# Another order of tasks and PSUM banks for a software-pipelined two-layer kernel on one core

## The reference, cut to what matters

```
xn = layernorm(x)
s  = tanh(beta * (spin + global + softmax(spin W_J spin^T) spin)),  spin = xn W_spin + b
g  = silu(sigmoid(xr W_r) * (relu(xk W_k)^2 W_v)),                  xr, xk mix a token with the one before
x  = x + s * g
xn = layernorm(x)
s  = retention over 16 heads (decaying causal scores, row sums of |scores|, rms norm), gated, W_o
g  = silu(soft mixture of 8 experts x 64 slots: logits, two softmaxes, slots, w1, gelu, w2, combine)
x  = x + s * g
```

## Time and profile before

| | us |
|---|---|
| median of 3 runs | 1090.27 (1090.27 to 1090.41) |
| the profiled execution | 1089.83 |
| its span, first to last instruction | 1088.0 |
| TensorE, VectorE, ScalarE, GpSimd busy | 1048.5, 919.0, 806.6, 387.3 |
| mean granted TensorE clock, of 2.4 GHz | 0.995 |

### The profile page before, as it was taken

How to read it: one execution, slowest core, us unless ns; L and a number is a source line. 1 busy time by engine, 2 the same in 40 slices (tenths; PEclk the granted TensorE clock), 3 DMA queues, 4 the chain that set the end, 5 groups by cost and what they waited for, 6 DMA issues and landing times.

```text
span 1088.0 us, 27272 instructions
## 1 busy us (share of the span) xinstructions
PE 1048.5 (96%) x10244; PEld 828.0 (76%) x10244; DVE 919.0 (84%) x1818; ACT 806.6 (74%) x1434; POOL 387.3 (36%) x555
## 2 busy tenths in 40 slices
PE   5799999999999999999999999999999999999997
PEld 3478787787878778787786877778787787877866
DVE  3788888988889888997988889888998888989785
ACT  4487877778777786877778777887777868777775
POOL 2432533334343332433335233343433324333240
PEclk9899999999999999999999999999999999999999
DMA  6000000000000000000000000000000000000000
GB/s 257 11 11 2 11 11 2 21 2 11 11 2 21 2 11 11 3 20 2 21 1 12 11 2 20 2 11 11 2 21 2 15 7 11 12 1 12 2 11 11
DMA packets 18463, 16.85 MB, mean 15 GB/s; under 512 B 800, under 2 KB 17440, under 8 KB 18080
## 3 DMA queue, kind: packets, MB, share of 16 engines
q1 hardware_dynamic: 18336, 15.12, 4.3%
HBM read 10.93 MB, written 4.19 MB: 14 GB/s over the span
## 4 chain that ended last, share of the span: by engine, by line
PE 90%; DVE 5%; issue 4%; POOL 1%; ACT 1%; DVEq 0%; POOLq 0%; ACTq 0%
PE bank L969 11%; PE bank L979 11%; PE bank L1023 10%; PE bank_s L1000 7%; PE bank L989 6%; PE bank L960 5%; PE bank L930 5%; PE bank L952 3%; PE bank L910 3%; PE bank L1038 3%; PE bank L825 3%; PE bank L1030 3%; PE bank L876 3%; PE bank L923 3%; PE bank L856 2%
## 5 line engine op out<-in xcount | busy, mean ns | idle before, releaser
L326 POOL TENSOR_TENSOR ret_abs<-ret_abs 128x512 f32<-128x512 f32 x128 | 168.3, 1315 | 435.9 <-ACT ret_abs L479 435.9
L659 DVE TENSOR_TENSOR ret<-bank_s,k_sb 128x1536 f32<-128x1536 f32 x128 | 224.1, 1751 | 5.0 <-PE bank L1023 2.2
L479 ACT ACTIVATE ret_abs<-ret 128x1536 f32<-128x1536 f32 x128 | 189.1, 1477 | 0.5 <-DVE ret L659 0.5
L474 ACT ACTIVATE hact<-hact 128x512 f32<-128x512 f32 x128 | 80.1, 626 | 86.5 <-DVE hact L728 86.1
L979 PE MATMUL bank<-w_sb,hact 128*128 128x128 f32 x1024 | 132.0, 277 | 0.0
L969 PE MATMUL bank<-slotsT,w_sb 128*128 128x128 f32 x1024 | 130.7, 278 | 0.9 <-ACT slotsT L469 0.9
L979 PEld LDWEIGHTS bank<-w_sb,hact 128*128 128x128 f32 x1024 | 124.1, 192 | 8.9 <-ACT hact L474 4.3
L969 PEld LDWEIGHTS bank<-slotsT,w_sb 128*128 128x128 f32 x1024 | 120.6, 192 | 10.2 <-issue 6.6
L1023 PE MATMUL bank<-ret,vrow 128*32 128x256 f32 (+1 forms) x2048 | 108.3, 329 | 0.0
L728 DVE TENSOR_TENSOR hact<-bank,v_sb 128x512 f32<-128x512 f32 x128 | 87.6, 685 | 11.7 <-PE bank L979 8.2
L333 POOL TENSOR_SCALAR dT<-dT,drec 128x256 f32<-128x256 f32 x128 | 64.5, 517 | 91.7 <-DVE drec L723 91.7
(11 more groups left out here) (143 smaller groups left out, 2307.1 us busy)
## 6 DMA issues: line engine op xcount, KB each, us to landing
x_sb<-x SPq DMA_DIRECT2D x16, 256.0 KB, 2.8
w_sb<-w SPq DMA_DIRECT2D x2, 2048.0 KB, 14.2
out<-attn SPq DMA_DIRECT2D x16, 256.0 KB, 2.3
v_sb<-vectors SPq DMA_DIRECT2D x1, 705.0 KB, 7.5
k_sb<-consts SPq DMA_DIRECT2D x1, 538.0 KB, 6.3
w_sb<-weights SPq DMA_DIRECT2D x1, 512.0 KB, 5.0
w_sb<-weights SPq DMA_DIRECT2D x1, 320.0 KB, 3.3
slot_sb<-slot_rows SPq DMA_DIRECT2D x1, 256.0 KB, 3.5
```

Of the source, the lines that this page charges most:

```text
L326: pool.tensor_tensor(both[:, :, P:SEQ], both[:, :, P:SEQ], both[:, :, SEQ:3 * P], ALU.add)\
L474: act.activation(hact[:, e % 2], hact[:, e % 2], ACT.Gelu).then_inc(ready["hg"].sem, 1)
L479: act.activation(ret_abs[:, q % MR], ret[:, q % MR], ACT.Abs).then_inc(ready["ab"].sem, 1)
L659: dve.tensor_tensor(ret[:, q % MR], bank_s[:, :, 0:3 * P], causal.unsqueeze(1).broadcast_to([P, Q, 3 * P]), ALU.mult)\
```

## The change

Both tables are written anew, and nothing else is touched: no function, no instruction and no transfer. In `ORDER` every engine's list has the same tasks as before in another sequence. Six tasks of TensorE change their age: quad 7, h 4, eo 2, eo 3 and h 5 go from 2 to 1, ms 2 from 1 to 2. On VectorE eoc 0, hb 3, ret 7, hb 4 and eoc 1, on ScalarE dsq 2 and hg 3 go from 2 to 1, and on GpSimd rstd2 from 1 to 0. `BANK` gives most tasks another bank. The new tables were laid out with longer durations for VectorE, ScalarE and GpSimd.

```diff
@@ -51,53 +51,53 @@
 ORDER = {
-    "PE": [("quad", 7, 2), ("h", 4, 2), ("eo", 2, 2), ("eo", 3, 2), ("h", 5, 2), ("h", 6, 2), ("eo", 4, 2),
-           ("h", 7, 2), ("eo", 5, 2), ("xn2T", 0, 1), ("g", 6, 2), ("g", 7, 2), ("qk", 0, 1), ("eo", 6, 2),
-           ("ms", 3, 2), ("eo", 7, 2), ("qk", 1, 1), ("gT", 0, 1), ("vg", 0, 1), ("xn3T", 0, 1), ("out", 0, 2),
-           ("quad", 0, 1), ("out", 1, 2), ("LT", 0, 1), ("LT", 1, 1), ("quad", 1, 1), ("LT", 2, 1), ("xnT", 0, 0),
-           ("LT", 3, 1), ("gT", 1, 1), ("vg", 1, 1), ("s", 0, 0), ("quad", 2, 1), ("g", 0, 1), ("g", 1, 1),
-           ("DT", 0, 1), ("e", 0, 0), ("global", 0, 0), ("r", 0, 0), ("o", 0, 2), ("quad", 3, 1), ("o", 1, 2),
-           ("k", 0, 0), ("ms", 0, 1), ("mxT", 0, 1), ("score", 0, 0), ("DT", 1, 1), ("score", 1, 0),
-           ("quad", 4, 1), ("g", 2, 1), ("g", 3, 1), ("PT", 0, 0), ("rB", 0, 1), ("DT", 2, 1), ("quad", 5, 1),
-           ("DT", 3, 1), ("srow", 0, 0), ("ms", 1, 1), ("PT", 1, 0), ("slots", 0, 1), ("slots", 1, 1),
-           ("v", 0, 0), ("local", 0, 0), ("h", 0, 1), ("quad", 6, 1), ("g", 4, 1), ("g", 5, 1), ("h", 1, 1),
-           ("h", 2, 1), ("h", 3, 1), ("eo", 0, 1), ("eo", 1, 1), ("ms", 2, 1)],
-    "DVE": [("eoc", 0, 2), ("hb", 3, 2), ("rx", 2, 2), ("ret", 7, 2), ("hb", 4, 2), ("eoc", 1, 2), ("hb", 5, 2),
-            ("xn2", 0, 1), ("hb", 6, 2), ("hb", 7, 2), ("stat", 0, 0), ("xn3", 0, 1), ("den", 3, 2), ("ug", 3, 2),
-            ("eoc", 2, 2), ("rx", 3, 2), ("qkc", 0, 1), ("eoc", 3, 2), ("qkc", 1, 1), ("vgc", 0, 1), ("z", 0, 2),
-            ("gated", 0, 2), ("ret", 0, 1), ("z", 1, 2), ("xn", 0, 0), ("LTm", 0, 1), ("gated", 1, 2),
-            ("ret", 1, 1), ("LTm", 1, 1), ("mx", 0, 1), ("LTm", 2, 1), ("vgc", 1, 1), ("mix", 0, 0), ("zg", 0, 2),
-            ("drec", 0, 1), ("mx", 1, 1), ("ret", 2, 1), ("den", 0, 1), ("gbias", 0, 0), ("mx", 2, 1),
-            ("ug", 0, 1), ("drec", 1, 1), ("attn", 0, 2), ("ret", 3, 1), ("attn", 1, 2), ("rx", 0, 1),
-            ("rmax", 0, 1), ("drec", 2, 1), ("LTm", 3, 1), ("sg", 0, 2), ("smax", 0, 0), ("smax", 1, 0),
-            ("drec", 3, 1), ("ret", 4, 1), ("den", 1, 1), ("ug", 1, 1), ("x2", 0, 2), ("cs", 0, 1), ("ka", 0, 0),
-            ("rx", 1, 1), ("cs", 1, 1), ("cs", 2, 1), ("srowc", 0, 0), ("ret", 5, 1), ("srec", 0, 0), ("rv", 0, 0),
-            ("cs", 3, 1), ("field", 0, 0), ("hb", 0, 1), ("rvg", 0, 0), ("prod", 0, 0), ("x1", 0, 0),
-            ("ret", 6, 1), ("hb", 1, 1), ("stat2", 0, 0), ("ug", 2, 1), ("den", 2, 1), ("hb", 2, 1)],
-    "ACT": [("dsq", 2, 2), ("hg", 3, 2), ("hg", 4, 2), ("ab", 7, 2), ("hg", 5, 2), ("ce", 3, 2), ("xn2Tc", 0, 1),
-            ("hg", 6, 2), ("usq", 3, 2), ("dsq", 3, 2), ("hg", 7, 2), ("ln", 0, 2), ("gTb", 0, 1), ("rs", 0, 2),
-            ("xn3Tc", 0, 1), ("LTc", 0, 1), ("zt", 0, 2), ("LTc", 1, 1), ("ab", 0, 1), ("LTc", 2, 1),
-            ("xnTc", 0, 0), ("ab", 1, 1), ("LTc", 3, 1), ("DTe", 0, 1), ("gTb", 1, 1), ("sT", 0, 0), ("DTe", 1, 1),
-            ("usq", 0, 1), ("Dc", 0, 1), ("eTc", 0, 0), ("ab", 2, 1), ("tr", 0, 0), ("dsq", 0, 1), ("DTe", 2, 1),
-            ("kr", 0, 0), ("sgT", 0, 0), ("ab", 3, 1), ("Dc", 1, 1), ("DTe", 3, 1), ("P", 0, 0), ("P", 1, 0),
-            ("usq", 1, 1), ("PTc", 0, 0), ("rBc", 0, 1), ("Dc", 2, 1), ("dsq", 1, 1), ("Dc", 3, 1), ("ab", 4, 1),
-            ("ce", 0, 1), ("slc", 0, 1), ("ce", 1, 1), ("PTc", 1, 0), ("slc", 1, 1), ("tv", 0, 0), ("ab", 5, 1),
-            ("ce", 2, 1), ("sp", 0, 0), ("hg", 0, 1), ("hg", 1, 1), ("usq", 2, 1), ("ab", 6, 1), ("hg", 2, 1)],
-    "POOL": [("add", 6, 2), ("rstd2", 0, 1), ("rnorm", 0, 1), ("add", 7, 2), ("rstd", 0, 0), ("km", 0, 1),
-             ("km", 1, 1), ("km", 2, 1), ("add", 0, 1), ("mixa", 0, 0), ("add", 1, 1), ("dn", 0, 1), ("km", 3, 1),
-             ("dn", 1, 1), ("add", 2, 1), ("km", 4, 1), ("km", 5, 1), ("add", 3, 1), ("dn", 2, 1), ("km", 6, 1),
-             ("km", 7, 1), ("dn", 3, 1), ("add", 4, 1), ("add", 5, 1)],
+    "PE": [("h", 6, 2), ("ms", 2, 2), ("eo", 4, 2), ("h", 7, 2), ("eo", 5, 2), ("xn2T", 0, 1), ("g", 6, 2),
+           ("g", 7, 2), ("xn3T", 0, 1), ("qk", 0, 1), ("qk", 1, 1), ("eo", 6, 2), ("ms", 3, 2), ("eo", 7, 2),
+           ("LT", 0, 1), ("quad", 0, 1), ("out", 0, 2), ("out", 1, 2), ("LT", 1, 1), ("gT", 0, 1), ("xnT", 0, 0),
+           ("vg", 0, 1), ("quad", 1, 1), ("gT", 1, 1), ("LT", 2, 1), ("o", 0, 2), ("vg", 1, 1), ("LT", 3, 1),
+           ("s", 0, 0), ("DT", 0, 1), ("quad", 2, 1), ("g", 0, 1), ("g", 1, 1), ("mxT", 0, 1), ("e", 0, 0),
+           ("k", 0, 0), ("quad", 3, 1), ("DT", 1, 1), ("rB", 0, 1), ("ms", 0, 1), ("DT", 2, 1), ("o", 1, 2),
+           ("score", 0, 0), ("global", 0, 0), ("score", 1, 0), ("quad", 4, 1), ("g", 2, 1), ("g", 3, 1),
+           ("PT", 0, 0), ("r", 0, 0), ("DT", 3, 1), ("quad", 5, 1), ("srow", 0, 0), ("PT", 1, 0), ("v", 0, 0),
+           ("slots", 0, 1), ("slots", 1, 1), ("local", 0, 0), ("ms", 1, 1), ("h", 0, 1), ("h", 1, 1),
+           ("quad", 6, 1), ("g", 4, 1), ("g", 5, 1), ("eo", 0, 1), ("h", 2, 1), ("eo", 1, 1), ("h", 3, 1),
+           ("quad", 7, 1), ("eo", 2, 1), ("h", 4, 1), ("eo", 3, 1), ("h", 5, 1)],
+    "DVE": [("hb", 5, 2), ("xn2", 0, 1), ("rx", 2, 2), ("hb", 6, 2), ("xn3", 0, 1), ("eoc", 2, 2), ("hb", 7, 2),
+            ("stat", 0, 0), ("ug", 3, 2), ("qkc", 0, 1), ("den", 3, 2), ("qkc", 1, 1), ("xn", 0, 0), ("rx", 3, 2),
+            ("eoc", 3, 2), ("ret", 0, 1), ("z", 0, 2), ("gated", 0, 2), ("z", 1, 2), ("LTm", 0, 1), ("LTm", 1, 1),
+            ("mx", 0, 1), ("vgc", 0, 1), ("drec", 0, 1), ("ret", 1, 1), ("gated", 1, 2), ("attn", 0, 2),
+            ("zg", 0, 2), ("vgc", 1, 1), ("LTm", 2, 1), ("mx", 1, 1), ("mix", 0, 0), ("mx", 2, 1), ("drec", 1, 1),
+            ("drec", 2, 1), ("ret", 2, 1), ("rmax", 0, 1), ("den", 0, 1), ("ug", 0, 1), ("ret", 3, 1),
+            ("rx", 0, 1), ("LTm", 3, 1), ("attn", 1, 2), ("sg", 0, 2), ("gbias", 0, 0), ("smax", 0, 0),
+            ("drec", 3, 1), ("smax", 1, 0), ("ka", 0, 0), ("ret", 4, 1), ("ug", 1, 1), ("srec", 0, 0),
+            ("cs", 0, 1), ("cs", 1, 1), ("den", 1, 1), ("srowc", 0, 0), ("rv", 0, 0), ("cs", 2, 1), ("ret", 5, 1),
+            ("x2", 0, 2), ("rvg", 0, 0), ("field", 0, 0), ("cs", 3, 1), ("hb", 0, 1), ("prod", 0, 0), ("rx", 1, 1),
+            ("hb", 1, 1), ("x1", 0, 0), ("stat2", 0, 0), ("ret", 6, 1), ("hb", 2, 1), ("eoc", 0, 1), ("den", 2, 1),
+            ("hb", 3, 1), ("ret", 7, 1), ("hb", 4, 1), ("ug", 2, 1), ("eoc", 1, 1)],
+    "ACT": [("ab", 7, 2), ("hg", 4, 2), ("hg", 5, 2), ("ce", 3, 2), ("xn2Tc", 0, 1), ("hg", 6, 2), ("usq", 3, 2),
+            ("xn3Tc", 0, 1), ("hg", 7, 2), ("dsq", 3, 2), ("ln", 0, 2), ("rs", 0, 2), ("LTc", 0, 1), ("LTc", 1, 1),
+            ("zt", 0, 2), ("gTb", 0, 1), ("DTe", 0, 1), ("xnTc", 0, 0), ("ab", 0, 1), ("gTb", 1, 1), ("LTc", 2, 1),
+            ("ab", 1, 1), ("DTe", 1, 1), ("LTc", 3, 1), ("DTe", 2, 1), ("sT", 0, 0), ("Dc", 0, 1), ("usq", 0, 1),
+            ("ab", 2, 1), ("eTc", 0, 0), ("kr", 0, 0), ("dsq", 0, 1), ("Dc", 1, 1), ("rBc", 0, 1), ("ab", 3, 1),
+            ("DTe", 3, 1), ("sgT", 0, 0), ("P", 0, 0), ("Dc", 2, 1), ("P", 1, 0), ("usq", 1, 1), ("PTc", 0, 0),
+            ("tr", 0, 0), ("Dc", 3, 1), ("PTc", 1, 0), ("ab", 4, 1), ("dsq", 1, 1), ("slc", 0, 1), ("tv", 0, 0),
+            ("ce", 0, 1), ("slc", 1, 1), ("ab", 5, 1), ("ce", 1, 1), ("sp", 0, 0), ("ce", 2, 1), ("hg", 0, 1),
+            ("hg", 1, 1), ("usq", 2, 1), ("hg", 2, 1), ("ab", 6, 1), ("hg", 3, 1), ("dsq", 2, 1)],
+    "POOL": [("rnorm", 0, 1), ("add", 6, 2), ("add", 7, 2), ("rstd", 0, 0), ("km", 0, 1), ("km", 1, 1),
+             ("km", 2, 1), ("km", 3, 1), ("dn", 0, 1), ("mixa", 0, 0), ("add", 0, 1), ("add", 1, 1), ("km", 4, 1),
+             ("dn", 1, 1), ("dn", 2, 1), ("km", 5, 1), ("km", 6, 1), ("add", 2, 1), ("add", 3, 1), ("dn", 3, 1),
+             ("add", 4, 1), ("add", 5, 1), ("km", 7, 1), ("rstd2", 0, 0)],
 }
 
 
-BANK = {("DT", 0): 1, ("DT", 1): 0, ("DT", 2): 1, ("DT", 3): 0, ("LT", 0): 1, ("LT", 1): 3, ("LT", 2): 1,
-        ("LT", 3): 2, ("PT", 0): 0, ("PT", 1): 2, ("e", 0): 3, ("eo", 0): 0, ("eo", 2): 2, ("eo", 4): 3,
-        ("eo", 6): 0, ("g", 0): 2, ("g", 2): 3, ("g", 4): 2, ("g", 6): 2, ("gT", 0): 2, ("gT", 1): 0,
-        ("global", 0): 0, ("h", 0): 3, ("h", 1): 0, ("h", 2): 1, ("h", 3): 3, ("h", 4): 0, ("h", 5): 1,
-        ("h", 6): 0, ("h", 7): 1, ("k", 0): 0, ("local", 0): 1, ("mxT", 0): 3, ("o", 0): 3, ("o", 1): 1,
-        ("out", 0): 2, ("out", 1): 0, ("qk", 0): 1, ("qk", 1): 3, ("r", 0): 1, ("rB", 0): 2, ("s", 0): 1,
-        ("score", 0): 1, ("score", 1): 2, ("slots", 0): 0, ("slots", 1): 3, ("srow", 0): 1, ("v", 0): 0,
-        ("vg", 0): 0, ("vg", 1): 3, ("xn2T", 0): 0, ("xn3T", 0): 1, ("xnT", 0): 3}
+BANK = {("DT", 0): 2, ("DT", 1): 3, ("DT", 2): 0, ("DT", 3): 1, ("LT", 0): 0, ("LT", 1): 3, ("LT", 2): 0,
+        ("LT", 3): 3, ("PT", 0): 0, ("PT", 1): 1, ("e", 0): 2, ("eo", 0): 0, ("eo", 2): 1, ("eo", 4): 0,
```

(6 more changed lines are left out.)

## The result

The new tables are faster: 1070.11 us median (1069.80 to 1070.99, 5 runs) against 1090.27 (1089.97 to 1090.41, 5 runs), a ratio of 0.982 with a 95% interval of 0.980 to 0.983. The step of the prediction that failed is one term of its sum, the 0.65 us a period that it added for stalls. The profiled execution took 1069.80 for a span of 1068.0.

A forecast was written before the change was run, and what follows sets the result against it. The prediction took TensorE's own work as the bound: 14 periods of 65.0 us plus 165.4 at the edges gave a span of 1075.4, plus 2.3 made 1077.7 us, with a range from 1071 to 1088.

The forecast's parts named there:

- the source of the gain: TensorE's wait at DT0 for dT from GpSimd, 0.90 us a period, was to go whole.
- the floor: TensorE's slots plus changes of tile size in one period, without stalls: 64.37 us in the new order.
- The edges: Time outside the fourteen periods (first pair, last full step, tail): 166.8 us before, less 1.4, so 165.4.
- New period: 64.37 + 0.25 + 0.2 + 0.2 = 65.0: New period in us: floor, kept small pieces, a stall at (a) and one at (b).
- The 0.25: Kept per period from 0.45 us of small TensorE pieces without a known cause; bounds 0 and 0.45.
- (a): Last pair's second-layer tail: xn meets km0 to km3, out0 waits for eoc3; 0.2 us a period, bounds 0 and 1.2.
- (b): Stretch from 20.9 to 31 of the period: VectorE meets GpSimd's adds ahead of mxT; 0.2 us, bounds 0 and 1.2.
- No stall of its own: Rival: xn slips between the km and (b) holds; a period of 64.6, 1072 us; chance 0.15.
- The wait that only moves: Rival: (a) at its upper bound, period 66.0, 1091.7 us; half of that gives 1083; chance 0.13 in all.
- slower: Rival: at (b) VectorE comes 2.5 us late and mxT waits; a period of 66.9, 1104 us; chance 0.10.
- rival 3: Same as slower: mixa holds gated1, add0 zg, add1 mx1, km4 or add1 mix, 0.7 to 0.9 each; chance 0.10.
- rival 2: Same as The wait that only moves: every meeting in (a) and (b) held in full; 1091.7 us; chance 0.13.

The follow-up runs named there:

- e2: Old kernel with one entry of VectorE's list moved, drec 0 ahead of mix: 1075.94 us, ratio 0.987.
- e7: New kernel with drec 0 moved behind zg in VectorE's list: 1118.31 us.
- e9: New kernel with h 1 moved between quad 6 and g 4, ten changes of tile size a period instead of nine: 1073.18 us.
- e10: New kernel with xnT moved behind quad 1 and LT 2 behind o 0: 1072.40 us.
- e8: New kernel with xn moved behind eoc3 instead of ahead of rx3, away from km0 to km3: 1070.22 us.
- e1: Old kernel with four entries of BANK changed (eo 2, h 4, h 5, h 6): 1086.53 us, ratio 0.9975.
- e5: New kernel with xn's four VectorE instructions issued a second time into a spare tile: 1084.07 us.
- e6: New kernel with one more VectorE maximum (0.6 us) ahead of mx2: 1079.32 us.
- e4: Old kernel's ORDER with the whole new BANK: 1344.89 us in one run.
- e3: Old kernel with both the four changed BANK entries and drec 0 ahead of mix: 1073.59 us, ratio 0.985.

## Why the prediction was right and wrong

**Right: the source of the gain.** DT0's wait goes, whole, because drec0 no longer lies behind a mix that an add holds. e2 shows it alone: 0.97 us a period from one entry. e7 shows it in reverse, with GpSimd's queue as the amplifier.

**Right: the floor.** 64.37 was added up from slots; the new kernel runs at 64.43, with TensorE busy throughout. The 0.06 between them belong to `global`, two products of two columns: the task behind it is 0.08 longer, score1 in the new order (1.04 us from start to start, 0.96 in the old), r0 in the old (0.97, and 0.89 in the new). In the trace its second weight load starts 0.08 us late, and its second product with it. I had that in neither sum. e9 and e10 confirm the price of a change of tile size, 0.20, and of a transposition behind it, 0.05 less.

**The edges: right as a sum, with luck.** 165.4 was forecast and 165.6 found. But pair 0's x1 was to end 0.35 earlier and ends at 29.23 where it was 28.84. And between 28 and 44 us the mean granted clock was 0.79 in this execution and 0.68 in that of the old kernel; it was 0.68 in e8, whose slots0 of pair 0 starts 0.55 later. So the start differs between executions by as much as the terms that I had for it.

**Wrong: the line "New period: 64.37 + 0.25 + 0.2 + 0.2 = 65.0".** Its three terms for stalls come to 0.65; over the fourteen periods 0.09 was found, 0.06 of it in each of the later ones, and that is the price of `global`. 14 x (65.0 - 64.46) = 7.6 us is the whole of the difference between 1077.7 and 1070.1.

- The 0.25 was what I kept of the 0.45 "in small pieces I can't tie to a cause". They have causes. Bank claims whose reader ends 0.14 to 0.19 us ahead make 0.21 (eo2, xn2T with the slot before it, eo0, h4); e1 shows 0.165 of it, and that eo0's 0.05 is of the same kind is read from its slot alone. ms2 behind den2 makes 0.10, `global` 0.08, and DT0's wait was 0.96 and not 0.90. Only the 0.08 of `global` is in the new order too. The others go with the places that cause them. The trace of before could have told: the end of the bank's last reader stands 0.14 (eo2), 0.15 (xn2T), 0.17 (eo0) and 0.19 us (h4) ahead of the slot, and den2's end 0.06 ahead of ms2. I had kept a piece without a line in the list of waits as if it came with TensorE. In the later periods of the new order the closest claim is g4's, 0.20 ahead; a few early ones stand at 0.15 (h4, eo4 and score0 of pair 1), and the second period, with 64.71, is the longest. My own walk counted 0.1 from reader to TensorE; for a bank claim 0.2 is right.
- The 0.2 of (a) was put in although, by the walk, out0 is late only if VectorE and GpSimd take full turns; the 0.2 of (b) although every margin was positive, as "less than my steps are sure to". Both measured zero. For what TensorE waits for there, the walk was good to 0.2 us, but for the full turns: eoc3 at 12.5 of the period (12.4 without, 13.2 with full turns), zg to 25.5 (25.3), mx2 at 29.4 (29.3), ret2 at 31.2 (31.2), eTc at 33.2 (33.25), Dc1 at 34.5 (34.6). e8 shows that (a) had nothing to give. e5 and e6 show that both places are real: they cost 0.94 and 0.58 us a period once VectorE is made later by some 1.4 and 0.6.

**The rivals.** "No stall of its own", with 0.15, came true, at 1070.1 and not 1072, since it too carried the 0.25. The wait that only moves, and slower, did not. Of the four collisions that rival 3 wanted three are there, gated1 (0.5 us longer), zg (0.75) and mix (0.2), and mx1 keeps its 0.68; xn lost 0.3 and not the 0.85 of full turns, since each engine gets in between two instructions of the other. The Trainium skill's rule ("SBUF — State Buffer", section "Who interferes with whom") that the pair of ports is held for a whole instruction agrees with (b), though the page says it of VectorE's two-port modes, and of an instruction with two inputs in SBUF only that it contends: zg starts 0.88 us ahead of the end of an add and takes 0.75 longer, a km starts together with mx1, which takes 0.68, and takes 0.54 longer. It speaks of one instruction, and rival 2 took it for a row of them.

## What to carry to other kernels

When one engine is the bound and works to the beat, add up its slots first: the distance between period and sum is all that an order can give, and here a single entry (e2) held some seven tenths of it. A piece that is a few hundredths longer than its like may be a wait even if the engine counts as busy; look for what ended 0.2 us or less ahead of it. And if a walk through the new order shows room everywhere, forecast the floor and put the doubt into the range, not a little stall at each tight place.

## What the runs showed of the hardware that I had not expected

- A bank claim costs TensorE nothing if its reader ends 0.20 us or more ahead of the slot (g4 in the new kernel, r0 in the old). A reader that ends 0.14 to 0.15 ahead has held TensorE, by 0.07 us in the old kernel (eo2, xn2T) and by up to 2.3 in e4; at 0.17 and 0.19 ahead the old kernel lost 0.05 and 0.02, while o1 at 0.19 to 0.20 lost nothing in e2 and e3 and 0.03 in e10. For an operand the distance is smaller: dn0 0.09 ahead of DT0 (e2, e3) and mx2 0.17 ahead of mxT (e10) cost nothing, and eoc3 stood 0.10 ahead of out0 where TensorE waited for it (e5). Why the two differ is not known.
- Stalls of TensorE can cost a second time. In e7, with 2.2 us of waiting a period in front of g0 and g1, the clock stayed at 1.00 for six periods and then fell to 1.2 GHz for a part of each, which made a period 1.4 us longer with no further wait. What set it off in the seventh period is not known.
